# Routing weights of a mixture-of-experts stage turned by 4-byte transfers instead of TensorE transposes, and the summed output turned one expert later

## The chip, the cores and the metric

The kernel runs on one core of one Trainium2 chip. The metric is the device time in microseconds. The profile comes from one execution on the same core; its durations are what the working below uses.

## The reference

For 16 batches of 512 rows of 128 numbers, all in fp32: a layer norm with scale and shift, causal attention with 16 heads of 64, a gated residual, a second layer norm, and then a mixture of 8 experts. Only the last part is touched here:

```python
logits = xf @ Wr + br                                  # 8 experts
topv, _ = lax.top_k(logits, 2)
masked = where(logits >= topv[:, 1:2], logits, -inf)
weights = softmax(masked)                              # [tokens, 8], two of them not zero
h = gelu(einsum('td,edh->eth', xf, W1) + b1)           # 128 -> 512
expert_out = einsum('eth,ehd->etd', h, W2) + b2        # 512 -> 128
out = einsum('etd,te->td', expert_out, weights)
x = x + gb * out
```

## The kernel before

There are two stages, one after the other: attention for all 16 batches (to about 1349 us of the profiled execution), then the experts for all 16 batches. Each engine has its own program, written out by hand: a first batch, a loop over batches 1 to 14, and a last batch. Semaphores alone order the engines; within an engine the order is that of the code.

In the expert stage the activations are kept transposed: 128 features on the partitions, 512 tokens (4 tiles of 128) along a row. TensorE runs, for each expert e of a batch, `first_layer(b, e)` (12 matmuls of 512 columns, L891 to L893: each product is split into a high and a low part) and then `second_layer(b, e - 1)` (12 matmuls, L904 to L906). ScalarE (ACT) applies the gelu chunk by chunk (L1027) and rounds two of four chunks (L1035). VectorE (DVE) rounds the other two (L1144), makes the low parts (L1146), and weighs the output of the expert before (`weigh_expert`, L1159): the PSUM result plus its bias, times the row of routing weights of that expert, `w_rows[:, e, :]`, which has to stand on all 128 partitions. GpSimd (POOL) adds up the weighted outputs (L965). At the second expert of the next batch ACT scales the sum (`gate_sum`, L1014), TensorE turns it back to tokens on partitions (`sum_T`, L913), DVE adds the residual (`finish`, L1168) and SP stores it (L1231).

The next batch is prepared during the present one: `norm_stats` at e = 1 and `norm_rows` at e = 2 on DVE, `norm_T` at e = 3 and `router_logits` at e = 4 on TensorE, `choose` at e = 4 and `weights` at e = 5 on DVE. The last operation of `weights` (L1125) writes `w_now`, with tokens on partitions and experts along the row.

Before the change these weights reach `w_rows` in four steps. `weights_T` (L880): four TensorE transposes at e = 6 into PSUM bank 6 (`w_now` is padded to 128 columns, and POOL clears it once). `weights_out` (L1007): an ACT copy of 8 partitions by 512 columns at e = 7. `lay_weights` on SP: one transfer to `w_kept` in HBM (L1220, 8 rows of 2 KB), a wait for its landing, and eight transfers (L1226), one for each expert, that read its row of `w_kept` for all 128 partitions. Each of these waits until the row of the batch before has been used. PSUM bank 6 also holds the result of `norm_T` and that of `sum_T`. On SP the order is: store of batch b - 1, then `lay_weights(b + 1)`.

Of the kernel before, what the change touches and what calls it, by code (L numbers as in the profile page):

```python
# [12 lines left out]
P = 128  # L13
# [31 lines left out]
def adaln_moe_kernel(nc, resid, W_Q, W_K, W_V, W_out, b_out, W1, b1, W2, b2, Wr, br, c_in, wmod, out):  # L45
# [10 lines left out]
    with ExitStack() as ctx:  # L56
# [730 lines left out]
        with ExitStack() as pb:  # L787
            def sbb(name, shape, dt=F32):
                return sb(name, shape, dt, pb)
# [20 lines left out]
            w_now = sbb("w_now", [P, NT, P])  # L810
            w_sum = sbb("w_sum", [P, NT])
            w_rsum = sbb("w_rsum", [P, NT])
            w_T = sbb("w_T", [E, S])
# [10 lines left out]
            hT_bank, wT_bank, out_bank = banks[:, 6, :], banks[:, 6, :], banks[:, 6, :]  # L824
# [14 lines left out]
            def expert(b, e):  # L839
# [4 lines left out]
            w_hi_ok, w_split_ok, w_now_clear = sem("w_hi_ok"), sem("w_split_ok"), sem("w_now_clear")  # L844
            r_stat, r_mv, r_eps, r_rstd, r_xn = (sem(f"r_{n}") for n in ("stat", "mv", "eps", "rstd", "xn"))
            r_T_ps, r_full, r_hi, r_lo = (sem(f"r_{n}") for n in ("T_ps", "full", "hi", "lo"))
            r_logit_ps, r_shift, r_exp, r_w, r_wT_ps, r_wT = (
                sem(f"r_{n}") for n in ("logit_ps", "shift", "exp", "w", "wT_ps", "wT"))
# [12 lines left out]
            with nc.Block() as block:  # L861
                @block.tensor
                def _(pe):
# [12 lines left out]

                    def weights_T(b):
                        pe.wait_ge(r_w, b + 1)
                        for t in range(NT):
                            mm = pe.transpose(wT_bank[:, t * P:(t + 1) * P], w_now[:, t, :], ident[:, :])  # L880
                        mm.then_inc(r_wT_ps, 1)
# [35 lines left out]
                    def body(b, first, last):  # L917
                        for e in range(E):
# [3 lines left out]
                            if e == 0 and first:  # L922
                                weights_T(0)
# [6 lines left out]
                            if e == 1 and not first:  # L930
                                sum_T(b - 1)
# [4 lines left out]
                            if not last and e == 6:  # L936
                                weights_T(b + 1)
# [10 lines left out]
                def _(pool):  # L948
# [27 lines left out]

                    pool.memset(w_now[:, :, :], 0.0).then_inc(w_now_clear, 1)
# [4 lines left out]
                def _(act):  # L982
# [18 lines left out]

                    def weights_out(b):
                        act.wait_ge(r_wT_ps, b + 1)
                        if not isinstance(b, int) or b > 0:

                            act.wait_ge(w_written, 16 * b)
                        act.activation(w_T[:, :], wT_bank[0:E, :], ACT.Copy).then_inc(r_wT, 1)  # L1007
# [29 lines left out]
                    def body(b, first, last):  # L1037
                        for e in range(E):
# [9 lines left out]
                            if e == 0 and first:  # L1048
                                weights_out(0)
                            if e == 4 and not last:  # L1050
                                h_evac(b + 1)
                            if e == 7 and not last:
                                weights_out(b + 1)
# [21 lines left out]
                def _(dve):  # L1075
# [40 lines left out]
                    def weights(b):  # L1116
# [5 lines left out]
                        if isinstance(b, int) and b == 0:  # L1122

                            dve.wait_ge(w_now_clear, 1)
# [144 lines left out]
```

## Time and profile before

| | us |
|---|---|
| time, median of 3 runs (lowest, highest) | 2116.58 (2116.27, 2116.94) |
| time of the profiled execution | 2116.83 |
| its span, first to last instruction | 2115.0 |
| attention stage, about | 1349 |
| expert stage, about | 766 |
| one batch of the loop in the expert stage | 46.25 |

The span is the time between the first and the last instruction; 1.8 us of the profiled execution lie around it. Busy times of engines are over the whole span and mix both stages, so the working below reads the expert stage by itself. A matmul of 512 columns shows some 390 ns because matmuls are pipelined; how many the engine gets through is read from the distance between their starts.

### The profile page before, as it was taken

The page shows a single profiled execution, that of the slowest core. Times are in us where ns is not written, and L with a number is a line of the kernel's source. Part 1 is how long each engine was busy: PE and PEld are TensorE (multiplying, and loading weights), DVE is VectorE, ACT ScalarE, POOL GpSimd, SP SyncE. Part 2 cuts the span into 40 slices and gives each one's busy share as a digit, 9 for nine tenths or more (in the row PEclk, how much of TensorE's full clock was granted, in tenths as well). Part 3 has the DMA queues.
Part 4 walks back from the last instruction along what each step waited for, and adds up shares of the span by engine and source line. Part 5 has one row for each costly group of instructions (what it writes and reads, how often), then busy time and mean ns, then how long its engine had stood idle before and what let it go on. Part 6 is the DMA issues. An engine that isn't in the chain of part 4 may idle for free. (4 is left out here: it accounts for less than half of the span.)

```text
span 2115.0 us, 46428 instructions
## 1 busy us (share of the span) xinstructions
PE 2016.3 (95%) x12751; PEld 1556.6 (74%) x12751; DVE 1691.4 (80%) x4517; ACT 1535.3 (73%) x3749; POOL 722.1 (34%) x1215
## 2 busy tenths in 40 slices
PE   4999999999999999999999999799999999999998
PEld 3777777777777776777777777478888888888887
DVE  5878777778778778778787787599888888988887
ACT  4878778778778777777777787477777777777775
POOL 2434443344443444343443443122222222222222
PEclk9999999999999999999999999899999999999999
DMA  3000000000000000000000000311111121111111
GB/s 108 21 1 1 0 0 0 0 0 0 0 0 0 0 0 0 0 0 0 0 0 0 0 1 1 113 48 51 45 45 45 56 69 50 50 45 45 45 59 37
DMA packets 41933, 49.46 MB, mean 23 GB/s; under 512 B 3177, under 2 KB 23713, under 8 KB 41889
## 3 DMA queue, kind: packets, MB, share of 16 engines
q1 hardware_dynamic: 41632, 48.41, 7.3%
q0 software_dynamic: 256, 0.53, 0.2%
q8 instruction: 20, 0.33, 0.1%
q14 instruction: 25, 0.20, 0.0%
HBM read 44.47 MB, written 4.46 MB: 23 GB/s over the span
## 5 line engine op out<-in xcount | busy, mean ns | idle before, releaser
L347 POOL TENSOR_SCALAR probs<-probs,rdenom 128x512 f32<-128x512 f32 (+3 forms) x1024 | 522.4, 532 | 742.3 <-DVE rdenom L710 742.3
L580 ACT ACTIVATE probs<-probs,neg_max 128x512 f32<-128x512 f32 (+3 forms) x1024 | 561.8, 550 | 204.8 <-DVE neg_max L701 204.8
L1027 ACT ACTIVATE hidden<-banks,b_cols 128x512 f32<-128x512 f32 x512 | 348.4, 685 | 198.5 <-PE banks L893 174.8
L701 DVE CUSTOM_DVE_ANT_0 probs<-banks,mask_w 128x512 f32<-128x512 f32 (+3 forms) x1024 | 433.5, 487 | 52.5 <-PE banks L410 50.5
L1146 DVE TENSOR_TENSOR hid_lo<-hidden,hid_hi 128x512 fp32r<-128x512 f32 x512 | 386.7, 763 | 67.7 <-ACT hid_hi L1035 55.4
L694 DVE COPY probs_T<-banks 128x512 f32<-128x512 f32 x384 | 262.2, 683 | 151.5 <-PE banks L436 149.6
L436 PE MATMUL banks<-ident,probs 128*128 128x128 f32 x2560 | 348.6, 275 | 0.5 <-DVE z_lo L714 0.5
L436 PEld LDWEIGHTS banks<-ident,probs 128*128 128x128 f32 x2560 | 293.4, 141 | 52.4 <-DVE neg_max L701 12.0
L965 POOL TENSOR_TENSOR acc<-acc,y_w 128x512 f32<-128x512 f32 x112 | 155.1, 1385 | 489.6 <-DVE y_w L1159 489.6
L451 PE MATMUL banks<-probs_T,v_sb 128*64 128x512 f32 (+3 forms) x2048 | 303.9, 439 | 10.4 <-DVE neg_max L701 5.4
L451 PEld LDWEIGHTS banks<-probs_T,v_sb 128*64 128x64 f32 x2048 | 139.1, 136 | 157.9 <-issue 123.3
L410 PE MATMUL banks<-k_hi,q_hi 64*128 64x512 f32 (+3 forms) x1024 | 184.4, 349 | 41.1 <-DVE k_lo L682 28.3
L891 PE MATMUL banks<-h_hi,w_hi 128*128 128x512 f32 x512 | 207.3, 405 | 3.6 <-DVE w_lo L1132 2.6
L904 PE MATMUL banks<-hid_hi,w_hi 128*128 128x512 f32 x512 | 199.9, 390 | 1.9 <-DVE w_lo L1132 1.9
L893 PE MATMUL banks<-h_lo,w_hi 128*128 128x512 f32 x512 | 201.0, 393 | 0.0
L892 PE MATMUL banks<-h_hi,w_lo 128*128 128x512 f32 x512 | 200.4, 391 | 0.0
L905 PE MATMUL banks<-hid_hi,w_lo 128*128 128x512 f32 x512 | 199.9, 390 | 0.0
L906 PE MATMUL banks<-hid_lo,w_hi 128*128 128x512 f32 x512 | 199.8, 390 | 0.0
L580 ACT ACTIVATION_READ_ACCUMULATOR probs<-probs,neg_max 128x1 f32 x1024 | 192.6, 188 | 0.0
L410 PEld LDWEIGHTS banks<-k_hi,q_hi 64*128 64x128 f32 x1024 | 100.4, 184 | 104.6 <-issue 69.4
L410 PE MATMUL banks<-k_hi,q_lo 64*128 64x512 f32 (+3 forms) x1024 | 169.6, 318 | 0.0
L410 PE MATMUL banks<-k_lo,q_hi 64*128 64x512 f32 (+3 forms) x1024 | 169.5, 319 | 0.0
(138 smaller groups left out, 3408.0 us busy)
## 6 DMA issues: line engine op xcount, KB each, us to landing
w_rows<-w_kept SPq DMA_DIRECT2D x128, 256.0 KB, 4.0
x_all<-in_L_attn_resid_dram SPq DMA_DIRECT2D x16, 256.0 KB, 2.8
out_dram<-y_result SPq DMA_DIRECT2D x16, 256.0 KB, 2.3
w_raw<-in_L_ffn_W_dram SPq DMA_DIRECT2D x12, 256.0 KB, 3.9
hidden<-in_L_ffn_W_dram SPq DMA_DIRECT2D x4, 256.0 KB, 5.8
v_sb<-in_L_attn_W_Q_dram SPq DMA_DIRECT2D x1, 512.0 KB, 5.2
v_sb<-in_L_attn_W_K_dram SPq DMA_DIRECT2D x1, 512.0 KB, 8.0
v_sb<-in_L_attn_W_V_dram SPq DMA_DIRECT2D x1, 512.0 KB, 11.4
```

Source lines behind the costliest of these rows:

```text
L347: pool.tensor_scalar(part, part, rdenom[:, p % 2, 4 * h + r:4 * h + r + 1], 1.0, ALU.mult, ALU.mult)\
L410: mm = pe.matmul(S_BANK[u][h][:, at:at + n], q[own, p % 2, rows], k[own, p % 2, 0:n], start=start, stop=stop)
L436: mm = pe.transpose(T_BANK[u][:, at:at + P], probs[:, p % 2, h, src:src + P], ident[:, :])
L451: mm = pe.matmul(z_bank[h * DH:(h + 1) * DH, c * P:S], v_sb[:, c, hc:hc + DH], probs_T[:, h, KEY_AT[c]:KEY_AT[c] + n], start=(c == 0), sto ...
L580: act.activation(part, part, ACT.Exp, bias=neg_max[:, p % 2, col:col + 1], scale=-1.0, accum_out=denom[:, p % 2, col:col + 1]).then_inc(p_ ...
L694: dve.tensor_copy(dst, src).then_inc(t_dve, 1)
L701: dve.tensor_tensor_reduce(out=probs[:, p % 2, h, at:at + n], in0=S_BANK[u][h][:, col:col + n], in1=mask_w[:, 512 - n:512], scale=-SCALE, ...
L891: pe.matmul(banks[:, c, :], w1_hi[:, e, cols], h2_hi[:, :], start=True, stop=False)
L892: pe.matmul(banks[:, c, :], w1_lo[:, e, cols], h2_hi[:, :], start=False, stop=False)
L893: pe.matmul(banks[:, c, :], w1_hi[:, e, cols], h2_lo[:, :], start=False, stop=True)\
L1027: act.activation(hidden[:, e % 2, c, :], banks[:, c, :], ACT.Gelu, bias=b1_cols[:, e * HC + c:e * HC + c + 1]).then_inc(hid, 1)
L1146: dve.tensor_tensor(hid_lo[:, e % 2, c, :], full, hi.bitcast(F32), ALU.subtract)\
```

## The change

`weights_T` and `weights_out` go, with their semaphores, the clearing of `w_now` and its padding. SP waits for the last operation of `weights` itself and issues four transfers, one for each tile of 128 tokens, that write `w_now` to `w_kept` with the two indices exchanged: every element is a run of 4 bytes in HBM, 1024 runs in each transfer. Before DVE writes `w_now` again it waits until the four transfers of the batch before have landed. The eight transfers to `w_rows` stay as they are. Apart from that, `sum_T` on TensorE and `finish` on DVE move from e = 1 to e = 2; `gate_sum` on ACT stays at e = 1.

```diff
-            w_now = sbb("w_now", [P, NT, P])
+            w_now = sbb("w_now", [P, NT, E])
-            w_T = sbb("w_T", [E, S])
...
-                    def weights_T(b):
-                        pe.wait_ge(r_w, b + 1)
-                        for t in range(NT):
-                            mm = pe.transpose(wT_bank[:, t * P:(t + 1) * P], w_now[:, t, :], ident[:, :])
-                        mm.then_inc(r_wT_ps, 1)
...
-                            if e == 0 and first:
-                                weights_T(0)
...
-                            if e == 1 and not first:
+                            if e == 2 and not first:
                                 sum_T(b - 1)
...
-                            if not last and e == 6:
-                                weights_T(b + 1)
...
-                    pool.memset(w_now[:, :, :], 0.0).then_inc(w_now_clear, 1)
...
-                    def weights_out(b):
-                        act.wait_ge(r_wT_ps, b + 1)
-                        if not isinstance(b, int) or b > 0:
-                            act.wait_ge(w_written, 16 * b)
-                        act.activation(w_T[:, :], wT_bank[0:E, :], ACT.Copy).then_inc(r_wT, 1)
...
-                            if e == 0 and first:
-                                weights_out(0)
...
-                            if e == 7 and not last:
-                                weights_out(b + 1)
...
-                            dve.wait_ge(w_now_clear, 1)
-                        dve.tensor_tensor(w_now[:, :, 0:E], kept[:, :, :], rsum, ALU.mult).then_inc(r_w, 1)
+                        if not isinstance(b, int) or b > 0:
+                            wait_alone(dve, w_written, 64 * b)
+                        dve.tensor_tensor(w_now[:, :, :], kept[:, :, :], rsum, ALU.mult).then_inc(r_w, 1)
...
-                            if e == 1 and not first:
+                            if e == 2 and not first:
                                 finish(b - 1, isinstance(b, int) and b == 1)
...
-                        sp.wait_ge(r_wT, b + 1)
-                        sp.dma_start(w_kept[ds(b, 1)].rearrange("b e s -> e (b s)"), w_T[:, :]).then_inc(w_written, 16)
-                        sp.wait_ge(w_written, 16 * (b + 1))
+                        sp.wait_ge(r_w, b + 1)
+                        with nc.allow_non_contiguous_dma("expert rows of the routing weights"):
+                            for t in range(NT):
+                                sp.dma_start(w_kept[ds(b, 1), :, t * P:(t + 1) * P].rearrange("b e p -> p (b e)"),
+                                             w_now[:, t, :]).then_inc(w_written, 16)
+                        sp.wait_ge(w_written, 64 * (b + 1))
```

## Rows read from the trace of the kernel before

**Rows 1.** Busy time of each engine in one batch of the loop

```profile
core 0: us, PE busy (x) PEld busy (x) DVE busy (x) ACT busy (x) POOL busy (x), PEclk, DMA share, GB/s
1593.50:1639.75 46.25, 46.14 (x214) 38.02 (x213) 41.36 (x83) 33.36 (x56) 10.94 (x9) 1.00 0.16 51
```

**Rows 2.** TensorE's timeline around the transposes of the routing weights

```profile
start us, us, engine line op out<-in xcount [idle before <-releaser]
1590.94 0.39 PE L905 MATMUL banks<-hid_hi,w_lo 128*128 128x512 f32 x1
1591.17 0.39 PE L906 MATMUL banks<-hid_lo,w_hi 128*128 128x512 f32 x1
1591.40 0.60 PE L880 MATMUL banks<-ident,w_now 128*128 128x128 f32 x4
1591.76 0.47 PE L891 MATMUL banks<-h_hi,w_hi 128*128 128x512 f32 x1
1592.07 0.39 PE L892 MATMUL banks<-h_hi,w_lo 128*128 128x512 f32 x1
```

**Rows 3.** TensorE's timeline around the transposes of the sum

```profile
1607.98 0.39 PE L906 MATMUL banks<-hid_lo,w_hi 128*128 128x512 f32 x1
1608.48 0.66 PE L913 MATMUL banks<-ident,acc_gated 128*128 128x128 f32 x4
1608.89 0.48 PE L891 MATMUL banks<-h_hi,w_hi 128*128 128x512 f32 x1
1609.20 0.39 PE L892 MATMUL banks<-h_hi,w_lo 128*128 128x512 f32 x1
```

**Rows 4.** Chain of waits over ten batches of the loop

```profile
engine line waited for: us in total, times, longest us
PEld banks L913 <- ACT acc_gated L1014: 5.3, 10, 0.5
```

**Rows 5.** SP's timeline of one batch

```profile
1594.06 0.32 SPq L1220 DMA_DIRECT2D w_kept<-w_T  x1
1595.70 10.24 SPq L1226 DMA_DIRECT2D w_rows<-w_kept  x8
1612.83 0.40 SPq L1231 DMA_DIRECT2D out_dram<-y_result  x1
```

**Rows 6.** DVE's timeline: weights made, and first used

```profile
1588.82 0.84 DVE L1125 TENSOR_TENSOR w_now<-kept,w_rsum 128x32 f32<-128x32 f32 x1
...
1610.08 0.74 DVE L1159 SCALAR_TENSOR_TENSOR acc<-banks,b_cols,w_rows 128x512 f32<-128x512 f32 x1
```

**Rows 7.** Landing times of the transfers of the weights' rows, whole span

```profile
DMA to landing us min/median/max: 3.0/4.0/6.8
```

**Rows 8.** DMA traffic 1612 to 1617 us, the store alone (512-byte rows)

```profile
DMA packets 528, 0.26 MB, mean 52 GB/s; under 512 B 16, under 2 KB 528, under 8 KB 528
q1 hardware_dynamic: 528, 0.26, 18.4%
```

**Rows 9.** DMA traffic 1594.0 to 1595.6 us, the write of `w_kept` alone

```profile
DMA packets 16, 0.02 MB, mean 10 GB/s; under 512 B 8, under 2 KB 8, under 8 KB 16
q1 hardware_dynamic: 16, 0.02, 5.7%
```

**Rows 10.** DVE's timeline around `finish` and the rows of the norm

```profile
1611.95 0.69 DVE L1168 TENSOR_TENSOR y_result<-banks,x_all 128x512 f32<-128x512 f32 x1
...
1616.55 2.12 DVE L1096 TENSOR_SCALAR xn<-x_all,meanvar,rstd 128x128 f32 x4
1618.59 0.68 DVE L1146 TENSOR_TENSOR hid_lo<-hidden,hid_hi 128x512 fp32r<-128x512 f32 x1
```

**Rows 11.** TensorE's timeline at the norm's transposes

```profile
1619.89 0.60 PE L867 MATMUL banks<-ident,xn 128*128 128x128 f32 x4
```

**Rows 12.** Timeline of the first batch

```profile
1363.96 0.19 DVE L1125 TENSOR_TENSOR w_now<-kept,w_rsum 128x32 f32<-128x32 f32 x1
1365.19 0.59 ACT L1007 ACTIVATE w_T<-banks 8x512 f32<-8x512 f32 x1 [3.73 <-PE banks L880]
...
1366.39 0.50 PE L891 MATMUL banks<-h_hi,w_hi 128*128 128x512 f32 x1 [0.54 <-ACT hidden L1027]
...
1371.46 0.68 PE L904 MATMUL banks<-hid_hi,w_hi 128*128 128x512 f32 x1 [1.92 <-DVE w_lo L1132]
...
1378.89 0.74 DVE L1159 SCALAR_TENSOR_TENSOR acc<-banks,b_cols,w_rows 128x512 f32<-128x512 f32 x1
...
1387.36 0.65 PE L867 MATMUL banks<-ident,xn 128*128 128x128 f32 x4 [0.43 <-DVE xn L1096]
```

More of the change, by code:

```diff
@@ L822, in adaln_moe_kernel @@
             y_banks = [banks[:, 4, :], banks[:, 5, :]]
-            hT_bank, wT_bank, out_bank = banks[:, 6, :], banks[:, 6, :], banks[:, 6, :]
+            hT_bank, out_bank = banks[:, 6, :], banks[:, 6, :]
             logit_bank = banks[:, 7, 0:NT * E]
@@ L843, in adaln_moe_kernel @@
             load_w = [[sem(f"load_w{layer}_{e}") for e in range(E)] for layer in (1, 2)]
-            w_hi_ok, w_split_ok, w_now_clear = sem("w_hi_ok"), sem("w_split_ok"), sem("w_now_clear")
+            w_hi_ok, w_split_ok = sem("w_hi_ok"), sem("w_split_ok")
             r_stat, r_mv, r_eps, r_rstd, r_xn = (sem(f"r_{n}") for n in ("stat", "mv", "eps", "rstd", "xn"))
             r_T_ps, r_full, r_hi, r_lo = (sem(f"r_{n}") for n in ("T_ps", "full", "hi", "lo"))
-            r_logit_ps, r_shift, r_exp, r_w, r_wT_ps, r_wT = (
-                sem(f"r_{n}") for n in ("logit_ps", "shift", "exp", "w", "wT_ps", "wT"))
+            r_logit_ps, r_shift, r_exp, r_w = (
+                sem(f"r_{n}") for n in ("logit_ps", "shift", "exp", "w"))
             w_written = sem("w_written")
@@ L1121, in weights @@
                         rsum = w_rsum[:, :].unsqueeze(2).broadcast_to([P, NT, E])
-                        if isinstance(b, int) and b == 0:
-                            dve.wait_ge(w_now_clear, 1)
-                        dve.tensor_tensor(w_now[:, :, 0:E], kept[:, :, :], rsum, ALU.mult).then_inc(r_w, 1)
+                        if not isinstance(b, int) or b > 0:
+                            wait_alone(dve, w_written, 64 * b)
+                        dve.tensor_tensor(w_now[:, :, :], kept[:, :, :], rsum, ALU.mult).then_inc(r_w, 1)
                         assert links[0] == CHAIN
```

## The prediction

> **What bounds the kernel now.** The change lies in the expert stage, so I leave the shares of the whole span aside and read one batch of the loop first. There TensorE is busy for 46.14 of 46.25 us, DVE for 41.36, ACT for 33.36, and the clock granted to TensorE is full [rows 1]. TensorE sets the pace, and DVE has 4.9 us a batch to spare. "Busy" says nothing on how dense that work is, so the next view is TensorE's timeline, and in it the distance between starts. Matmuls of 512 columns start 0.23 us apart [rows 2]. 192 of them make some 44 us, and the other 2 us or so are the four interruptions: turned norm, router, turned weights, turned sum. What the change can win is in the last two, and what it can lose is in whatever makes TensorE wait that does not do so now. In the chain of waits TensorE waits in the loop for one thing only, the gated sum [rows 4].
>
> **What goes: the transposes of the weights.** From the start of the last matmul before them (1591.17) to the start of the second one after them (1592.07) there are 0.90 us; without them it would be two steps, 0.45 us [rows 2]. The first matmul after a transpose starts its successor 0.31 us later and not 0.23; that is in the 0.90. So 0.45 us a batch. Nothing hides this: it is the engine that sets the pace. It occurs for 15 batches in the stage after the first; I count 14 here and treat the first two calls with the start below: 14 * 0.45 = 6.3 us.
>
> **What moves: the transposes of the sum.** The same measure is 1609.20 - 1607.98 = 1.22 us [rows 3]. The block has the same four transposes as that of the weights, so 0.90 of it is work and 0.32 is waiting for `acc_gated`. The chain of waits says 5.3 us in ten batches [rows 4], but that is idle time of the weight loads, part of which lies over a running matmul; I take the distance of starts. One expert later the gated sum has been ready for some 5 us, so the 0.32 go and the 0.90 stay: 15 * 0.32 = 4.8 us. The sixteenth call, after the last batch, stays where it is, with its wait.
>
> **What moves with it on DVE.** `finish` (0.69 us) leaves the place between the norm's statistics and the chunks of expert 2 and comes ahead of `norm_rows` [rows 10]. Its input is there: `sum_T` follows `second_layer(1)` by half a microsecond, and DVE comes to it only after `weigh_expert` (0.74). What could be late is `norm_T`: `xn` is complete at 1618.67 and TensorE wants it at 1619.89, 1.2 us later [rows 10, 11]. TensorE will want it 0.23 us earlier than now, counted from the expert before (0.68 earlier by the missing block and its wait, 0.45 later by the block that comes in), at about 1619.66. If nothing of the earlier relief on DVE survives, `xn` is ready at 1619.36, still 0.3 us in hand. So this costs nothing; if the 0.3 are gone too, the price is what is missing, at most the 0.32 just won. The store goes out one expert later; SP's next work waits for weights that come three experts later still, so nobody queues behind it. POOL's clearing of `w_now` and ACT's copy (0.57 to 0.59 us a batch) were beside TensorE's work and are worth nothing in the loop. The new wait on DVE ahead of L1125 is for transfers of a batch ago. It is passed at once and costs the few hundredths of an empty instruction, in a stretch that ends in idle time of DVE.
>
> **What is added: the 4-byte transfers.** This is the open price. Each of the four transfers has 1024 runs; over 16 DMA engines that is 64 runs, and 256 runs on each engine for the whole batch. The trace before has no such run. I bound it from both sides by packets on the same queue toward HBM. In the window with only the store, 528 packets took 18.4% of 16 engines * 5 us = 14.7 us: 28 ns each, for 512 bytes [rows 8]. In the window with only the write of `w_kept`, 16 packets took 5.7% of 16 * 1.6 = 1.46 us; if all of it is laid on the 8 rows of 2 KB it is 180 ns each [rows 9]. From below nothing but zero is certain. I take 28 ns, since a packet of 4 bytes has less to move than one of 512, and of the two it is the nearer in size. The Trainium skill ("DMA: Bandwidth & Descriptors", Rules for kernel authors) says that a strided last dimension lowers to one descriptor per element; no run of before shows it, and it agrees with the count of 256 that I have from the access pattern.
>
> The fixed part: one transfer issued at 1594.06, and the first row transfer issued 1.65 us later, with the landing in between [rows 5]. So the write takes W = 1.65 + 256 * 0.028 = 8.8 us, with the three further issues (0.32 each) hidden behind the packets of the first ones. The bounds are 1.65 + 0 to 1.65 + 256 * 0.18 = 47.7 us.
>
> Now the deadline. `w_now` is complete at 1589.66 and expert 0 of the next batch is weighed at 1610.08: 20.4 us [rows 6]. A row transfer takes 4.0 us to land, at worst 6.8 [rows 7]. 20.4 - 8.8 - 4.0 leaves 7.6 us, and 4.8 in the worst case. The other seven rows are wanted 5 to 6 us apart, and SP issues them every half microsecond as far as the rows of the batch before are used. So in the loop the transfers are hidden. The price of a run at which DVE begins to wait is (20.4 - 4.0 - 1.65) / 256 = 58 ns (47 with the slowest landing). Behind a waiting DVE stand `norm_stats`, `finish` and `norm_rows`, and for these TensorE waits after another 1.0 to 1.2 us [rows 10, 11]; the 0.77 us won in a batch are used up by a run of about 65 ns. Beyond that each further nanosecond costs 0.256 us a batch, 3.8 us in all.
>
> **The start.** In the first batch ACT stood 3.73 us in front of the copy, then TensorE waited 0.54 us for a gelu chunk and 1.92 us for a low part of W2 that came late behind it [rows 12]. These could shrink by about 2.5 us. But the first weights are tighter: `w_now` at 1364.15, plus 8.8, plus 5.7 for a landing beside the loads of W2 (an estimate between the median and the slowest) is 1378.7, and DVE weighed at 1378.89 [rows 12]. DVE is then held there as before, and TensorE was waiting on DVE behind it (0.43 us at L867) [rows 12]. So the relief at the start is mostly given back; with the transposes of the first two calls themselves I take 1.0 us, between 0 and 4.
>
> **Sum.** 6.3 + 4.8 + 1.0 = 12.1 us. 2116.83 - 12.1 = 2104.7 us; the profiled execution lies 0.25 us above the median, so 2104.5 to 2104.7. I say 2104.6, 0.57% less.
>
> **The rivals.**
> (A) The forecast: the runs are hidden, TensorE wins both blocks. From 11.1 (nothing at the start) to 15.1 (4 us at the start) it gives 2101.5 to 2105.5; with the loss of the sum's 0.32 it is 2109.5. Its own range is 2100 to 2110. For it: the margin of 4.8 to 7.6 us. Chance 0.75.
> (B) The write of the 4-byte runs takes the place of the wait removed: `weigh_expert(b + 1, 0)` waits on DVE, then `norm_T` on TensorE, once a batch. It decides from 65 ns a run. At the upper bound of 180 ns the rows land at 1589.66 + 47.7 + 4.0 = 1641.4, 31.3 us late; less 1.1 of slack and 0.77 of gain it is 29.4 us a batch, 441 us over 15 batches, and about 37 at the start: some 2595 us. At 80 ns it is 0.256 * 15 * 15 = 58 us more than before. For it: the write of few rows has the dearest packets of the two windows. Against: those carried 512 times the bytes. Chance 0.15. The Trainium skill ("DMA: Bandwidth & Descriptors", Specifications) speaks against the change here: below 512 bytes the engine does a read-modify-write. No row of before shows it. If that doubled the 28 ns, the write would take 1.65 + 256 * 0.056 = 16.0 us and the rows would land at 1609.7, 0.4 us before they are wanted: still (A), with the start some 7 us late on DVE.
> (C) The runs are a little dearer and only the start pays: at 45 to 60 ns W is 13 to 17 us, the first weighing is 4 to 8 us late, and of the 11.1 us some 3 to 7 stay: 2110 to 2114, and with the slowest landings the loop loses a part too, to 2120. Chance 0.10, half of it within 0.2% (4.2 us, about what a measurement of this kernel can tell from no change).
>
> **How the numbers follow.** The time is that of (A). The range 2099 to 2114 holds nearly all of (A) and more than half of (C), about 0.8; (B) is left out on the upper side. Faster by over 0.2% (below 2112.4): (A) and half of (C), 0.79. Within 0.2%: 0.06. Slower: (B), 0.15.
>
> **What the profile after would show.** Right: no rows of L880 and L1007; a batch of the loop at 45.5 us; a stretch of DMA with over 4000 packets that ends some 7 to 9 us after `w_now`; the first row transfer issued 9 us after L1125 and not 6; `sum_T` starting 0.23 us after the matmul before it; no wait of DVE at L1159 for a DMA. Wrong: `norm_T` waiting for `xn` would take away the second term; a wait of DVE at the acc row of L1159 for the rows' transfer is (B) in every batch, (C) in the first alone; SP's issues of the four transfers growing from 0.3 to several microseconds would say that the queue, not the packets, sets W. The prediction fails altogether if a 4-byte run costs over 65 ns.

## The result, and the profile after

The changed kernel took 2243.62 us (median of 6 runs, 2239.35 to 2255.0) against 2116.76 us for the kernel before: ratio 1.0602, 95% interval 1.0578 to 1.0626. It is 127 us slower where 12 us less were forecast. The forecast time, its range and its sign were wrong; rival (B) is what happened.

The busy times of two batches of the loop, with the columns of [rows 1]:

```profile
core 0: us, PE busy (x) PEld busy (x) DVE busy (x) ACT busy (x) POOL busy (x), PEclk, DMA share, GB/s
1576.34:1630.12 53.78, 47.66 (x209) 38.73 (x208) 40.38 (x82) 32.59 (x55) 11.49 (x9) 0.94 0.56 44
1630.12:1684.87 54.75, 48.21 (x209) 38.51 (x208) 40.87 (x82) 32.59 (x55) 11.49 (x9) 0.94 0.53 43
```

A batch takes 54.25 us on average (13 distances between the first writes of two batches) and took 46.25. TensorE is no longer busy all the time, its granted clock is below full, and the DMA share has grown from 0.16 to 0.56 for as many bytes a batch as before (fewer GB/s over a longer batch). The share adds up the times of all packets, and those of one engine can overlap. SP's timeline of one batch, which answers to [rows 5], says with what:

```profile
start us, us, engine line op out<-in xcount [idle before <-releaser]
1576.34 2.32 SPq L1198 DMA_DIRECT2D w_kept<-w_now  x4
1601.83 4.47 SPq L1205 DMA_DIRECT2D w_rows<-w_kept  x8
1611.70 0.41 SPq L1210 DMA_DIRECT2D out_dram<-y_result  x1
```

From the issue of the first short transfer to that of the first row transfer there are 25.5 us; before they were 1.65. In the 14 loop batches of this trace it is 23.8 to 27.3, mean 25.6. SP's own part, the issue of the four, is only 2.3 us. What the DMA engines do in this stretch (1576 to 1602 us), in the columns of [rows 8]:

```profile
DMA packets 4160, 0.02 MB, mean 1 GB/s; under 512 B 4160, under 2 KB 4160, under 8 KB 4160
q1 hardware_dynamic: 4160, 0.02, 87.2%
```

4160 packets are 4096 runs and 64 signals. Their 87.2% of 16 engines * 26 us make 363 us, 87 ns a packet where the prediction took 28. The price is not even. In two early microseconds (1577 to 1579) half of them pass, at 0.95 * 16 * 2 / 2248 = 14 ns each:

```profile
DMA packets 2248, 0.01 MB, mean 4 GB/s; under 512 B 2248, under 2 KB 2248, under 8 KB 2248
q1 hardware_dynamic: 2248, 0.01, 95.0%
```

Then the engines are held, but not until the end. Here is the same stretch in two parts, in the columns of [rows 1]:

```profile
1576.34:1593.50 17.16, 17.16 (x77) 14.09 (x76) 13.72 (x22) 10.08 (x18) 4.23 (x3) 1.00 1.32 1
1593.50:1601.80 8.30, 8.30 (x40) 6.87 (x39) 3.44 (x6) 7.15 (x14) 0.00 (x0) 1.00 0.00 0
```

The share of 1.32 is that of overlapping packets. The last packet has ended at 1593.4, and for the next 8.3 us no DMA engine has one, while SP still waits for the landing of the four transfers. Over the 14 loop batches the last packet ends 16.7 us after the first issue (15.7 to 17.6), and the row transfer follows 8.9 us later (7.0 to 10.9). So a third of the 25.6 us is not packets at all but the landing behind them.

How the delay reaches TensorE stands in the timelines of the same batch. DVE's:

```profile
1596.90 0.69 DVE L1122 TENSOR_TENSOR hid_lo<-hidden,hid_hi 128x512 fp32r<-128x512 f32 x1
1605.06 0.75 DVE L1135 SCALAR_TENSOR_TENSOR acc<-banks,b_cols,w_rows 128x512 f32<-128x512 f32 x1 [7.47 <-DMA w_rows<-w_kept]
```

And TensorE's:

```profile
1598.85 0.40 PE L899 MATMUL banks<-hid_lo,w_hi 128*128 128x512 f32 x1
1599.08 0.60 PE L906 MATMUL banks<-ident,acc_gated 128*128 128x128 f32 x4
...
1607.66 0.77 PE L897 MATMUL banks<-hid_hi,w_hi 128*128 128x512 f32 x1 [5.21 <-DVE hid_lo L1122]
1608.23 0.63 PE L898 MATMUL banks<-hid_hi,w_lo 128*128 128x512 f32 x1
1608.66 0.63 PE L899 MATMUL banks<-hid_lo,w_hi 128*128 128x512 f32 x1
```

DVE stands 7.5 us in front of the weighing of expert 0, as 1601.83 plus a landing of 3.2 us says. Behind it are the chunks of expert 2, and `second_layer(2)` on TensorE waits 5.2 us for them; the norm's transposes then wait 0.9 us for `xn`. The chain of waits over twelve batches of the loop (1547 to 2200 us) has the first two waits in every batch and the third in ten:

```profile
DVE acc L1135 <- DMA w_rows<-w_kept: 89.4, 12, 8.7
PE banks L897 <- DVE hid_lo L1122: 62.8, 12, 6.5
PE banks L866 <- DVE xn L1072: 9.7, 10, 1.3
```

That is 5.2 + 0.8 = 6.0 us of TensorE's time a batch. The rest of the longer batch is slower work, in which the clock has the largest part that these rows show. After the idle stretch the matmuls start 0.43 us apart and not 0.23, and the granted clock is at its lower level, 1.2 of 2.4 GHz, until 1611.2. Busy times by engine in two stretches, then the clock, the DMA share and GB/s:

```profile
1602.00:1608.00 6.00, 0.79 (x4) 0.40 (x3) 2.94 (x11) 1.99 (x4) 0.88 (x2) 0.71 0.70 217
1608.00:1610.00 2.00, 2.00 (x6) 1.52 (x6) 1.93 (x5) 0.00 (x0) 0.99 (x1) 0.50 0.86 322
```

Two lines of the timeline above show also what went as forecast: the block of the sum starts 0.23 us after the matmul before it (1599.08 - 1598.85), and was 0.50 in [rows 3].

### The profile page after: what moved, and what is told of

Read it like the earlier page. It is cut to its first block and busy times, and to the rows that moved or that the text cites. A ratio compares the mean times of both kernels' runs of the same rounds, so it can differ in the third digit from the quotient of the medians.

```text
span 2242.7 us, 46429 instructions
## 1 busy us (share of the span) xinstructions
PE 2047.5 (91%) x12687; PEld 1566.8 (70%) x12687; DVE 1683.6 (75%) x4517; ACT 1524.0 (68%) x3733; POOL 730.6 (33%) x1214
## 5 line engine op out<-in xcount | busy, mean ns | idle before, releaser
L1122 DVE TENSOR_TENSOR hid_lo<-hidden,hid_hi 128x512 fp32r<-128x512 f32 x512 | 377.3, 747 | 48.2 <-ACT hid_hi L1015 30.3
L897 PE MATMUL banks<-hid_hi,w_hi 128*128 128x512 f32 x512 | 213.3, 417 | 86.4 <-DVE hid_lo L1122 85.7
L410 PE MATMUL banks<-k_hi,q_hi 64*128 64x512 f32 (+3 forms) x1024 | 184.8, 350 | 40.8 <-DVE k_lo L682 28.4
L898 PE MATMUL banks<-hid_hi,w_lo 128*128 128x512 f32 x512 | 210.5, 411 | 0.0
L899 PE MATMUL banks<-hid_lo,w_hi 128*128 128x512 f32 x512 | 209.7, 410 | 0.0
L897 PEld LDWEIGHTS banks<-hid_hi,w_hi 128*128 128x128 f32 x512 | 103.1, 201 | 115.3 <-issue 76.4
```

Source lines behind the costliest of these rows:

```text
L410: mm = pe.matmul(S_BANK[u][h][:, at:at + n], q[own, p % 2, rows], k[own, p % 2, 0:n], start=start, stop=stop)
L897: pe.matmul(y_bank, w2_hi[:, e, c, :], hi, start=(c == 0), stop=False)
L898: pe.matmul(y_bank, w2_lo[:, e, c, :], hi, start=False, stop=False)
L899: mm = pe.matmul(y_bank, w2_hi[:, e, c, :], lo, start=False, stop=(c == HC - 1))
L1122: dve.tensor_tensor(hid_lo[:, e % 2, c, :], full, hi.bitcast(F32), ALU.subtract)\
```

## The experiments

Fourteen runs were made, in four groups; those of a group ran on the same chip. The kernel before took 2116.8 to 2117.1 us in each group.

**The move alone.** The kernel before with `sum_T` and `finish` at the third expert.

```diff
-                            if e == 1 and not first:
+                            if e == 2 and not first:
                                 sum_T(b - 1)
...
-                            if e == 1 and not first:
+                            if e == 2 and not first:
                                 finish(b - 1, isinstance(b, int) and b == 1)
```

> The kernel before with only the summed output turned one expert later; the weights are still turned on TensorE. Theory 1 (the transposes of the sum waited 0.32 us in each of 15 batches for the gated sum, and nothing else waits in their place): 4.8 us faster, about 2112.0. Rival (the wait comes back at the norm's transposes, since DVE now does the residual ahead of the norm's rows): no change within 1 us, with a wait at the norm's transposes in the chain of waits.

2112.65 us, ratio 0.998 (0.9971 to 0.9989), 4.2 us less. The batch of the loop went from 46.25 to 45.95 us, and TensorE waits for nothing in the loop:

```profile
core 0: us, PE busy (x) PEld busy (x) DVE busy (x) ACT busy (x) POOL busy (x), PEclk, DMA share, GB/s
1592.99:1638.93 45.94, 45.94 (x214) 38.12 (x213) 40.83 (x82) 33.35 (x56) 11.60 (x9) 1.00 0.16 52
```

The second term of the sum holds (46.25 - 45.95 = 0.30 us a batch against 0.32), and so does the argument that `xn` is in time.

**Wide runs in place of short ones.** All as changed, but the same bytes go out in 128 runs of 32 bytes a transfer. Experts and tokens are not exchanged.

```diff
-   sp.dma_start(w_kept[ds(b, 1), :, t * P:(t + 1) * P].rearrange("b e p -> p (b e)"), w_now[:, t, :])
+   sp.dma_start(w_kept[ds(b, 1), 2 * t:2 * t + 2, :].rearrange("b a (p e) -> (b a p) e", e=E), w_now[:, t, :])
```

> The changed kernel, but the four transfers write the same bytes in the order in which they stand in SBUF, in 128 runs of 32 bytes each (512 runs a batch and not 4096); experts and tokens are not exchanged, so every weight stands at another place. All else is as changed. Theory 1 (the whole loss comes from the number of short runs): the write takes 2 to 4 us, no wait of DVE for rows, batch of the loop about 45.5 us, 12 us faster than before, about 2104.7. Rival (the loss comes from the moved work or from writing so early beside other traffic): still slower than before.

2102.89 us, ratio 0.9933 (0.9919 to 0.9947), 13.9 us less than before. The write takes 3.25 us, and TensorE has no gap in one batch of the loop:

```profile
core 0: us, PE busy (x) PEld busy (x) DVE busy (x) ACT busy (x) POOL busy (x), PEclk, DMA share, GB/s
1584.11:1629.61 45.50, 45.50 (x210) 37.64 (x209) 40.77 (x82) 33.05 (x55) 11.75 (x9) 1.00 0.18 52
```

So what the change takes out and moves is worth 14 us, and the short runs alone turn this into a loss of 127.

**The same short runs, cut by expert.** One transfer for each expert, one in flight ahead, each row sent out as soon as its write has landed.

```diff
+   write(0)                       # w_kept[b, e, :] as "(t p) -> p t" from w_now[:, :, e], own semaphore
+   for e in range(E):
+       if e + 1 < E: write(e + 1)
+       wait_alone(sp, w_wrote[e], 16 * (b + 1))
+       ...                        # the wait for the old row, and the row transfer of expert e, as before
```

> The changed kernel with the same 4096 runs of 4 bytes a batch, but cut into eight transfers by expert, each expert's row sent to all partitions as soon as its own write has landed, with one write in flight ahead. Theory 1 (what hurts is that the first row waits for all 4096 runs): the first row lands some 8 to 10 us after the weights, later rows each some 3 us apart, under the 5.7 us between their uses; no wait on DVE; 11 to 12 us faster than before, 2105. Rival (writes of 4 bytes into one row of HBM collide more, or slow the row transfers behind them): the eight writes take 5 us and more each, and DVE waits for rows again; time between 2116 and 2240.

2108.16 us, ratio 0.9959 (0.9945 to 0.9972): faster than before by 8.7 us, less than the 11 to 12 expected, and the expected pace was wrong. The first row follows the weights after 8.3 us in the batch shown, but the writes keep SP waiting almost the whole batch. Its timeline:

```profile
1591.18 0.97 SPq L1199 DMA_DIRECT2D w_kept<-w_now  x2
1599.51 0.37 SPq L1209 DMA_DIRECT2D w_rows<-w_kept  x1
1600.06 0.37 SPq L1199 DMA_DIRECT2D w_kept<-w_now  x1
1600.66 0.37 SPq L1209 DMA_DIRECT2D w_rows<-w_kept  x1
1601.21 0.37 SPq L1199 DMA_DIRECT2D w_kept<-w_now  x1
1610.80 0.37 SPq L1209 DMA_DIRECT2D w_rows<-w_kept  x1
```

Two writes of 512 runs, 4 KB together, take 8 to 12 us, so 4096 runs take some 42 us (first write to last row, 38 to 46 in the loop) where four transfers by tile took 25. The deadline is met because each row has its own; in the ten loop batches looked at DVE once waited 1.0 us for a row. That the same 4096 runs take longer in this order was the first sign that their number alone is not what is paid for. The gain is smaller than expected because the first batch has no batch before it to hide in: DVE waits there 6.1 us for rows and landings, and from its weights to the next there are 43.8 us, against 37.6 with wide runs.

**Probes of the transfers by themselves.** The kernel before, with transfers from a constant tile on SP's queue, which idles in the attention stage, each group followed by a wait for its landing.

```diff
+   for name, pieces in probes:
+       for t in range(pieces):
+           sp.dma_start(*probe_of(name, t, ident[:, 0:E])).then_inc(p_sem[name], 16)
+       sp.wait_ge(p_sem[name], 16 * pieces * (r + 1))
```

> The kernel before, with probes on SP's queue in the attention stage, where that queue is idle: each a few transfers of 128 partitions by 8 numbers from a constant tile, then a wait for their landing; three times each. as_is: four transfers like those of the change. one, two: one or two of them. pad64, pad512: the same, every element 64 or 512 bytes from the next in HBM. near: 4-byte runs 8 bytes apart, in the order of SBUF. wide: runs of 32 bytes. sbuf: 4-byte runs into SBUF. back: 4-byte runs read from HBM into SBUF. Theory A (HBM takes short writes slowly, whatever their place): as_is, pad64, pad512 and near all 20 to 27 us, wide 3, sbuf and back under 8. Theory B (neighbouring elements in one block of HBM collide): as_is 25, pad64 and pad512 under 10. Theory C (every short run costs its engine some 90 ns anywhere): as_is, sbuf, back all 25. If a buffer takes the first 2000 runs, one is 3 us, two 6 us, as_is 25; if not, one is 7, two 13.

SP's timeline of the second round; a group that follows another under one name is in the same row:

```profile
156.87 40.69 SPq L358 DMA_DIRECT2D p_as_is<-ident  x7
213.38 9.05 SPq L358 DMA_DIRECT2D p_pad<-ident  x8
227.01 2.71 SPq L358 DMA_DIRECT2D p_near<-ident  x4
244.85 1.76 SPq L358 DMA_DIRECT2D p_wide<-ident  x4
247.69 2.80 SPq L358 DMA_DIRECT2D p_sbuf<-ident  x4
252.16 2.57 SPq L358 DMA_DIRECT2D p_back<-p_as_is  x4
```

From start to start, with the starts inside a row read in narrower windows:

| probe | runs | us, rounds 1, 2, 3 |
|---|---|---|
| as_is, four transfers as in the change | 4096 of 4 B | 16.1, 24.9, 23.8 |
| one of them | 1024 | 14.0, 14.8, 15.2 |
| two of them | 2048 | 16.9, 16.8, 16.2 |
| pad64, 64 B from element to element | 4096 | 6.9, 6.8, 7.4 |
| pad512 | 4096 | 7.3, 6.8, 6.7 |
| near, 8 B apart, in the order of SBUF | 4096 | 18.1, 17.8, 18.1 |
| wide, 32 B | 512 | 5.2, 2.8, 2.9 |
| sbuf, short runs into SBUF | 4096 | 4.5, 4.5, 4.5 |
| back, short reads from HBM | 4096 | 5.2, 5.1, not read |

Theory B is the one that these rows leave: the same 4096 short writes take 25 us side by side and 7 us when 64 bytes apart; reads from HBM and writes into SBUF take 4.5 to 5.2. So at the same count and the same size of run, the place in HBM makes the price. Who writes the neighbours doesn't matter much: in `near` the runs that share 64 bytes come from one partition, in as_is from 16, and `near` still takes 18 us. My guess about a buffer for the first 2000 runs failed as a forecast of the time: one transfer alone takes 15 us. But the DMA engines do pass its packets at once. Here is the second round of `one`, from its issue to 183.5 us:

```profile
DMA packets 1040, 0.00 MB, mean 2 GB/s; under 512 B 1040, under 2 KB 1040, under 8 KB 1040
q1 hardware_dynamic: 1040, 0.00, 26.9%
```

All 1040 packets end within 1.6 us, at 0.269 * 16 * 1.74 / 1040 = 7.2 ns each. From 183.5 to 196.5 us this queue has none, and the landing comes at 196.6. Nearly all of the 15 us lies behind the engines' last packet.

**The count kept, the neighbours taken away, in the kernel.** The 4096 short runs go 64 bytes apart into a buffer that nobody reads, and the four transfers of wide runs, from which the rows are read, come on top.

```diff
+   w_apart = nc.dram_tensor("w_apart", [B, E, S, 16], F32)
-   sp.dma_start(w_kept[ds(b, 1), :, t * P:(t + 1) * P].rearrange("b e p -> p (b e)"), w_now[:, t, :])
+   sp.dma_start(w_apart[ds(b, 1), :, t * P:(t + 1) * P, 0].rearrange("b e p -> p (b e)"), w_now[:, t, :])
+   ...                            # and the four wide transfers; SP waits for all eight
```

> The changed kernel with its 4096 runs of 4 bytes a batch, each now 64 bytes from the next in a buffer that nobody reads, and four transfers of 32-byte runs besides, from which the rows are read (so every weight stands at another place). SP waits for all eight. Theory B (neighbouring elements collide, the count of runs is cheap): the write takes 8 to 9 us, no wait of DVE, 2102 to 2105, though there are more runs than in the changed kernel. Theory A or C (a price for every run): the write takes 27 us and the time is 2240 to 2260.

2103.62 us, ratio 0.9939 (0.9924 to 0.9954). Both writes together take 7.8 us on average; on SP's timeline of one batch:

```profile
1629.95 2.29 SPq L1199 DMA_DIRECT2D w_apart<-w_now  x4
1632.42 2.00 SPq L1202 DMA_DIRECT2D w_kept<-w_now  x4
1637.68 7.99 SPq L1209 DMA_DIRECT2D w_rows<-w_kept  x8
```

**How near is near.** Probes again: 1024 runs with a growing distance in HBM.

```diff
+   p_at[name] = nc.dram_tensor(f"p_{name}", [E, S, k], F32)        # k = 1, 2, 4, 8, 16
+   sp.dma_start(p_at[name][:, t * P:(t + 1) * P, 0].rearrange("e p -> p e"), ident[:, 0:E])
```

> The kernel before, with probes on SP's idle queue in the attention stage as in the earlier run of probes. One transfer, then four, of 1024 runs of 4 bytes each, with 4, 8, 16, 32 and 64 bytes from one token's element to the next in HBM, so that 16, 8, 4, 2 and 1 of them fall into a block of 64 bytes; then one transfer of 1024 runs of 16 bytes side by side; three times each. Theory B with blocks of 64 bytes: one transfer takes 15 us at 4 bytes, about 8 at 8, 4 to 5 at 16, then 3 and under; with blocks of 32 bytes the floor is reached at 32. The 16-byte runs as the 16-byte spacing, 4 to 5. Theory A: 15 us at every spacing, against what the first probes showed at 64.

| bytes from element to element | one transfer, rounds 1, 2 | four transfers |
|---|---|---|
| 4 | 12.9, 15.6 | 22.7, 24.3 |
| 8 | 9.6, 9.3 | 15.0, 16.6 |
| 16 | 7.7, 7.4 | 13.0, 12.1 |
| 32 | 4.1, 3.6 | 7.6, 7.3 |
| 64 | 2.4, 2.4 | 7.0, 7.4 |
| 1024 runs of 16 B, side by side | 4.7, 3.4 | |

For one transfer the time falls at every step to 64 bytes, more slowly than the number of neighbours (16 bytes were expected at 4 to 5 us and took 7.5), and, by the earlier probes, not beyond. Four transfers are at their floor with 32 bytes already, so 64 bytes as the size of the block is not sharply shown. In the packets the steps don't appear: at 4 and at 64 bytes alike the 1040 packets of one transfer end 1.6 us after its issue. The landing follows 14.0 us later at 4 bytes (round 2) and 0.8 us later at 64. Side by side in wider runs is cheap.

**Runs of 16 bytes.** `w_now` is kept as expert by tile, one transfer writes 1024 runs of 16 bytes, and the rows come with another order of tokens, which DVE undoes as it reads.

```diff
-            w_now = sbb("w_now", [P, NT, E])
+            w_now = sbb("w_now", [P, E, NT])
+   sp.dma_start(w_kept[ds(b, 1)].rearrange("b e (p t) -> p (b e) t", p=P), w_now[:, :, :])
-                                                 scalar=b2_cols[:, e:e + 1], in1=w_rows[:, e, :],
+                                                 in1=w_rows[:, e, :].rearrange("q (p t) -> q t p", t=NT),
```

> The changed kernel with the tokens of a row of weights in another order: the weights are kept as expert by tile in each partition, so that one transfer writes 1024 runs of 16 bytes, and DVE reads each row with a stride of 16 bytes. Same result as the reference. Theory B (writes into the same small block of HBM wait for one another, so 4 of them in 64 bytes and not 16 cost a quarter): the write takes 4 to 6 us, no wait of DVE, 2102 to 2104. Theory A (HBM takes some 6 ns for every short write, whatever its place): 1024 runs take some 7 to 8 us, the same time. Rival (DVE's strided read costs more, or 16 bytes collide as 4 do): the write takes 15 us or DVE's weighing grows from 0.74 us, 2110 and more.

2128.08 us, ratio 1.0054 (1.004 to 1.0068), slower than before. The write takes 3.3 us, as theory B said; the rival's second half decided. A weighing whose row of weights is read with a stride of 16 bytes (the other operands in four pieces side by side) takes 1.13 us where the plain one takes 0.745, 8 * 0.385 = 3.1 us a batch on DVE, and TensorE waits for the next batch's `h_lo` 1.2 us a batch. The group of DVE's line over ten batches (1550 to 2010 us), with busy time and mean duration:

```profile
L1135 DVE SCALAR_TENSOR_TENSOR y_w<-banks,b_cols,w_rows 128x512 f32<-128x512 f32 x68 | 76.8, 1130 | 0.0
```

The chain of waits of the same stretch:

```profile
PE banks L884 <- DVE h_lo L1077: 12.2, 10, 1.3
```

**The change without the move.** `sum_T` and `finish` back at the second expert.

```diff
-                            if e == 2 and not first:
+                            if e == 1 and not first:
                                 sum_T(b - 1)
...                                                        # and finish likewise
```

> The changed kernel with the transposes of the sum and the residual back at the second expert. Theory 1 (TensorE stalls some 6 us a batch for DVE behind the late rows, and the moved block lies beside that): the deadline of the rows is counted from TensorE's pace, so the move is worth 0 to 5 us here, 2240 to 2250. Rival (the move made the loss, by putting the residual ahead of the norm's rows behind the late rows): 10 us and more faster than the changed kernel, under 2234.

2216.94 us, 27 us below the first measurement of the changed kernel, and outside what was expected. But its write took 23.5 us a batch and not 25.6. So both were run side by side on one chip, unaltered.

```diff
    # no edit: the changed kernel, and the one without the move
```

> The changed kernel again, unaltered, on the chip of the run after it, to see whether its distance of 27 us to the variant without the move (2216.9) is of the kernel or of the chip. Theory (the write took 2 us a batch less there, 23.5 and not 25.6 us, by the chip or by chance): both at the same time within 6 us. Rival (the move itself costs when the rows are late): 20 us and more above it again.

> The variant without the move again, beside the changed kernel. By the theory its write takes as long as there and the time is 0 to 6 us above that of the changed kernel; by the rival it is 20 us and more below it.

The changed kernel took 2210.27 us there, ratio 1.0438 (1.0418 to 1.0457), the one without the move 2214.58. With writes of 23.7 us in both, the batches are 52.25 and 52.76 us long. The 27 us came with the chip or the group of runs, not with the move. The variant is 4 us slower here, but the intervals of the two ratios overlap (1.0418 to 1.0457 and 1.044 to 1.0472), so what the move is worth behind late rows is not shown beyond that it costs nothing clear. The loss of the change is 93 us here and was 127 in the first measurement; the write is shorter here.

**Half of the short runs.** Two transfers as in the change (rows 1024 bytes apart), two wide.

```diff
+   flat = w_kept[ds(b, 1), 0:4, :].rearrange("b a (r s) -> (b a r) s", r=2)
+   dst = flat[:, t * P:(t + 1) * P].rearrange("e p -> p e")          # t < 2; t = 2, 3 in runs of 32 bytes
```

> The changed kernel, with two of the four transfers as they are in it (2048 runs of 4 bytes) and two in runs of 32 bytes (so weights stand at other places). Theory B (the time is that of the writes that follow one another in a block, 14 us for one transfer, 16 to 17 for two side by side): the write takes 16 to 17 us, the first row lands within 1 us of the moment at which DVE wants it, TensorE hardly waits, 2102 to 2107. A price for every run in proportion (half of 24 us): 12 to 13 us, no wait, 2103. Both say that the loss is gone though half of the short runs are left.

2105.04 us, ratio 0.9945 (0.993 to 0.996). Its write takes 11.7 us and TensorE does not wait in the loop. The loss is gone, as both readings said. The 11.7 us are near those of a price in proportion (12 to 13), not the 16 to 17 that I took from the probe. The packets end after 3.5 us on average, the landing takes the other 8.3.

**The distance of the rows.** Two further kernels: probes with other distances between the rows of two experts, and the changed kernel with 64 bytes of padding behind each row.

```diff
+   p_at[name] = nc.dram_tensor(f"p_{name}", [E, k], F32)            # k = 256, 512, 528, 544, 576, 1040
```
```diff
-            w_kept = nc.dram_tensor("w_kept", [B, E, S], F32)
+            w_kept = nc.dram_tensor("w_kept", [B, E, S + 16], F32)
```

> The kernel before, with probes on SP's idle queue in the attention stage: transfers of 1024 runs of 4 bytes, tokens side by side, with another distance between the rows of two experts: 1024, 2048, 2112 and 2304 bytes for one transfer; 1024, 2048 and 2112 for two; 2048, 2112, 2176, 2304 and 4160 for four; twice each. If only the 64-byte block counts, one transfer takes 13 to 15 us and four take 23 at every distance. Rival (the eight rows of a transfer also collide, because they lie a power of two apart, and the half that took 11.7 us had them 1024 bytes apart): the distances that are no power of two are clearly faster, under 10 us for four, and two at 1024 take 9 to 10 us against 16 at 2048.

> The changed kernel with 64 bytes of padding behind each row of weights in HBM (2112 bytes and not 2048 from expert to expert), all else the same, same result. If the power of two matters: the write takes under 15 us and the time is 2102 to 2106. If only the neighbours in a block of 64 bytes do: the write takes 23 to 25 us again, 2205 to 2245.

One transfer: 10.7 and 12.9 us at 1024 bytes (rounds 1, 2), 16.8 at 2048, 15.6 and 15.8 at 2112, 12.9 and 12.7 at 2304. Two: 12.8 and 13.0 at 1024, 18.5 and 19.0 at 2048, 18.6 and 18.0 at 2112. Four: 27.4 and 27.6 at 2048, 26.9 and 25.1 at 2112, 28 to 30 at 2176 and 2304, 36 at 4160 (one round). The padded kernel took 2286.79 us, ratio 1.0799 (1.0781 to 1.0817), with a write of 27.4 us. The rival with the power of two falls. The other expectation was missed too: 27.4 us and 2286.79 lie above its 23 to 25 and 2205 to 2245. But the probe of four transfers at the change's own 2048 bytes also took 27 us in this group, so it is the group that is slower, and the padding changes nothing that these runs can tell. Rows near each other are cheaper, which fits the 11.7 us in sign (12.8 in the probe against 18.5). So the neighbours within 64 bytes are not all that counts; why the distance of the rows counts, these runs don't say. A larger footprint in HBM by itself doesn't help: four transfers at 4160 bytes from row to row are the slowest, and with every element 64 bytes from the next they take 7 us.

**A version that reads where the change writes.** Wide runs out to HBM, one transfer that reads them back exchanged (4096 short reads, 8 rows written into SBUF), then the 8 rows to HBM as in the kernel before.

```diff
+   sp.dma_start(w_nat[ds(b, 1)].rearrange("b (t p) e -> p (b t) e", p=P), w_now[:, :, :])
+   sp.dma_start(w_T[:, :], w_nat[ds(b, 1)].rearrange("b s e -> e (b s)"))
+   sp.dma_start(w_kept[ds(b, 1)].rearrange("b e s -> e (b s)"), w_T[:, :])     # a wait behind each
```

> A version meant to beat both kernels. The weights go to HBM in the order of SBUF (512 runs of 32 bytes), one transfer reads them back with the two indices exchanged (4096 reads of 4 bytes, 8 rows of 2 KB written into SBUF), and one transfer writes these 8 rows to HBM as before the change; then the rows as always. Three landings follow one another on SP. Theory B (only short writes into one block of HBM collide, short reads don't): 2 to 3 us, then 5 to 9 us, then 1.7 us, some 11 us in all, no wait of DVE, 2102 to 2105. Rival (4096 short reads on 8 engines are as slow as the short writes): 20 us and more, 2150 and more.

2109.48 us, ratio 0.9964 (0.995 to 0.9978), 7.6 us faster than before, and 4.5 us above the 2102 to 2105 that were expected. In the loop it does all that was asked: 45.5 us a batch with 12.9 us from the first issue to the row transfers, on SP's timeline:

```profile
1590.26 0.41 SPq L1199 DMA_DIRECT2D w_nat<-w_now  x1
1592.08 0.77 SPq L1202 DMA_DIRECT2D w_T<-w_nat  x1
1601.54 0.32 SPq L1204 DMA_DIRECT2D w_kept<-w_T  x1
1603.19 4.43 SPq L1210 DMA_DIRECT2D w_rows<-w_kept  x8
```

The other 6 us it gives back in the first batch, where there is no batch before to hide in: TensorE waits 4.0 us there for a low part behind the late rows, and the distance from the first write to the second is 44.3 us against 38.1 with wide runs. It, the cut by expert and the move alone beat both kernels and compute all of the reference; 1.3 us lie between the first two, and their intervals overlap.

## Why the prediction was wrong, point by point

**Right: what bounds the kernel, and what the removed work is worth.** TensorE sets the pace, with four interruptions a batch. Forecast were 0.45 us for the transposes of the weights and 0.32 for the wait of the sum, 45.48 us a batch; wide runs give 45.50, and the move alone 45.95. Forecast in all were 12.1 us, measured 13.9 with the transfers out of the way. The missing part is the start: from the first batch's weights (the start of the last operation of `weights` on DVE) to the second's there were 40.8 us before and are 37.6 with wide runs. These 3.3 us are within the "0 to 4", and 2.3 above the 1.0 taken. The reason for taking little there was that DVE is "held there as before", and that is a misreading of [rows 12]: the row at 1378.89 names no wait, and DVE had worked without a gap right up to it. The landing of 5.7 us was too dear too. In the run with the 4096 runs apart the first write took 8.8 us, just as assumed; the rows landed 3.2 us after their issue, and DVE waited 0.5 us:

```profile
1376.20 0.75 DVE L1136 SCALAR_TENSOR_TENSOR acc<-banks,b_cols,w_rows 128x512 f32<-128x512 f32 x1 [0.54 <-DMA w_rows<-w_kept]
```

One small sum is off without effect: TensorE wants `norm_T` 0.32 us earlier and not 0.23 (0.77 less 0.45), and `xn` is still in time, as the move alone showed.

**Wrong: the write, W = 1.65 + 256 * 0.028 = 8.8 us, measured 25.6.** Two steps failed. The first is the price of a run: "I take 28 ns, since a packet of 4 bytes has less to move than one of 512, and of the two it is the nearer in size". If the fixed 1.65 us are kept, as the prediction's sum has it, measured are (25.6 - 1.65) / 256 = 94 ns in the first trace and 86 in the second. The second is the fixed part itself: "with the landing in between" was taken to stay at 1.65 us whatever was written. The packets take only some 16 of the 25.6 us, (16.7 - 0.9) / 256 = 62 ns a run with the first packet 0.9 us after the issue, which is under the break-even of 65 ns; it is the landing, 8.9 us behind the last packet, that carries the write past the deadline. A price per packet, even one read from these packets, would have missed this. The lower of the bounds was taken because only size had been compared. Size was the wrong axis: short writes 64 bytes apart cost (6.9 - 1.65) / 256 = 20 ns, inside what the choice assumed. What was not seen is that the exchanged order puts 16 tokens of one expert, one run at a time, into the same 64 bytes of HBM. No row of the trace before has two writes into one such block, so neither bound spoke of it; that the upper bound of 180 ns covers the result is luck of a wide bound.

**Right: the deadline and the break-even, but the range didn't follow them.** Weights to use were 20.4 us, a run of 58 ns makes DVE wait, one of 65 ns uses up the gain, each further nanosecond costs 3.8 us. With 94 ns this gives (94 - 65) * 3.8 = 110 us of loss; measured are 127. With 86 ns it gives 80, and measured are 93; with the 101 ns of the padded kernel 137, and measured are 170. The rule has the deadline right and the slope too small. In the batch shown DVE waits 7.5 us, where 25.5 + 4.0 - 20.4 says 9.1; the rows landed in 3.2 us and not in 4.0. With bounds of 0 and 180 ns and a break-even at 65, the 0.15 for rival (B) was too little for what the rows bore out.

**Not named: two amplifiers.** Behind the waiting DVE the prediction put only the norm's statistics and rows; what TensorE waits for first are the chunks of expert 2, 5.2 us, and the norm's `xn` adds 0.8. And TensorE's granted clock is lower after the idle stretch: 9 matmuls take 3.8 us (1607.66 to 1611.49) in place of 2.1. Over 13 batches of 54.25 us TensorE is busy for 48.2 and idle for 6.1, where wide runs have 45.5 us of work and no idle. So the 8.75 us that a batch is longer are 6.1 of waiting and 2.7 of the same work done more slowly; of the 2.7 the 9 matmuls show 1.8, and the rest isn't traced here.

**The count of descriptors, and the rule for short writes.** The Trainium skill ("DMA: Bandwidth & Descriptors", Rules for kernel authors) gives one descriptor per element for a strided last dimension; the trace after agrees, with 4160 packets. Its read-modify-write below 512 bytes (the same page, Specifications) pointed the right way, but as a price of every short run it isn't what the runs show: 32-byte runs and 4-byte runs 64 bytes apart are cheap. It was weighed as a doubling of the 28 ns, which was my estimate and not the page's.

**Still open.** What passes between the last packet and the landing, and why it takes 10 to 15 us for one transfer of 1024 runs alone and only 7 to 11 for four; why rows nearer to each other are cheaper; and why the same kernel's write took 25.6 us in one measurement and 23.7 in another, and 17 to 18 us in the first batch of each (21 in the padded kernel). That writes to one block of HBM wait for one another is the reading that fits the distances; nothing here looks into the memory itself.

## What to carry to other kernels

Before an exchange of indices is put into a store to HBM, look at which elements share 64 bytes there, and not at the size of a run alone: neighbours written one by one made 16 KB take 25 us. Don't price such a write by its packets alone: the landing, for which the reader waits, came up to 11 us after the last of them. Put the exchange on the reading side or into SBUF, or give each consumer its own short piece with its own deadline. And where the cover of a transfer is finite, price the miss (here 3.8 us for each nanosecond of a run) before the chance is set: a small gain beside a steep loss needs the unknown price bounded by rows of the same kind, or no forecast of the sign.

## What the runs showed of the hardware that was not expected

- 4096 writes of 4 bytes to HBM: 22.7 to 27.6 us side by side (16.1 in one first round), 6.7 to 7.4 us at 64 or 512 bytes; one transfer of 1024: 12.9 to 16.8 us at 4 bytes, 9.5 at 8, 7.5 at 16, 3.6 to 4.1 at 32, 2.4 at 64. The same number of reads from HBM took 5.2 us, of writes into SBUF 4.5 us.
- The DMA engines are done long before such a write has landed: one transfer of 1024 runs side by side has its last packet 1.6 us after the issue and lands after 14.8; in the changed kernel the landing came 7.0 to 10.9 us after the last packet. With 64 bytes from run to run it was 0.8 us for one transfer.
- Such a write takes another time from one measurement to the next: 25.6 and 23.7 us a batch in the same kernel, 2243.6 and 2210.3 us in all.
- DVE's weighing of 128 x 512 fp32 took 1.13 us with one operand at a stride of 16 bytes in SBUF, 0.745 without.
- TensorE's granted clock fell to its lower level within an idle stretch of 5.2 us (0.71 as the mean of 1602 to 1608 us) and stayed there for 3.6 us of dense work.
